# Projecting two blocks of h in each of the first 25 trips of the edge stage, and none in the later ones

## The chip, the cores and the metric

The kernel runs on one core of one Trainium2 chip. The metric is the device time of one execution in microseconds. The cores' engines are TensorE (PE; PEld is its weight load), VectorE (DVE), ScalarE (ACT), GpSimd (POOL) and SyncE (SP), each with its own queue of instructions, which runs in order.

## The reference

One layer of graph attention over N = 6250 nodes of 256 features and E = 200000 edges, sorted by destination, between two layer norms and a feed-forward part. What matters here:

```python
h = jnp.maximum(_layernorm(x, axis=-1), 0.0)
q, k, v = linear(h, wq, bq), linear(h, wk, bk), linear(h, wv, bv)
scores = jnp.sum(q[dst] * k[src], axis=-1) * scale + edge term
attn = softmax of scores over the edges of one dst
out = jax.ops.segment_sum(v[src] * attn[:, None], dst, num_segments=n)
h = layer_norm(h + out + linear(h, ws, bs), g1, b1)      # <- h + linear(h, ws, bs) is the residual
h = layer_norm(h + ffn(h), g2, b2)
return x + h
```

The destinations are `(6250 * uniform ** 2).astype(int)`, sorted. So they are crowded at low numbers: of the 49 blocks of 128 nodes the first holds 56 chunks of 512 edges and the last about 4.

## The kernel before

There are three parts: the first (to about 121 us) normalises x to h, writes h to memory (`h_rows`) and forms q; the edge stage (to about 2078 us) handles all edges; the last part turns the sums into the output.

The edge stage works on chunks of C = 512 edges, 4 tiles of 128. T = 391 chunks hold edges, TP = 392 with the pad. A step is one chunk together with one block of 128 nodes, so a chunk whose edges belong to two blocks takes two steps. A plan made at run time (`steps_tab`) lists the steps, 440 with two empty ones at the end, and the queues run them in 55 trips of U = 8, each trip being one turn of a loop (`eng.Fori(0, n)`) whose body has the eight steps written out. Because the edges are sorted there is one round (`rounds` = 1). Otherwise the same loops would run 49 rounds.

- GpSimd gathers the source rows of a chunk with four indirect DMAs (line 501), each started once a slot of the eight in `rows` is free (`slot_free`). It runs ahead of all others. The first eight chunks are gathered before the stage.
- SyncE waits until the four gathers of a chunk have landed and tells it by `chunk_landed` (L384); it then waits until an older chunk is used up and frees a slot (L388). It also loads the destinations (`dst_of`, L397).
- VectorE multiplies the gathered rows with the q of their destinations (L848, four tiles), takes the running maximum (L902), marks the edges of a block (L715) and adds a step's sums to `acc` (L861).
- ScalarE takes the exponentials (L629, L630), copies their transposes (L633) and prepares the mask of a later step (L596).
- TensorE, in a step: transposes of the exponentials (L1078), the expansion of q to the edges of step s + 2 in two halves (L1025), the spreading of the scores of step s + 1 (L1031), and last the sums of step s (L1091, eight matmuls). The second half of the expansion waits until the products of step s + 1 are done, and those wait for the landing of that step's chunk. So the sums of a step stand behind the landing of the next step's chunk.

Among the steps lies work that has nothing to do with edges: the residual r = h + (h ws + bs) of a block (the identity is added to ws beforehand). A turn of it is

- `turn_h` on TensorE (L1039): two transposes of a block of h, which was loaded before;
- `copy_hTe` on ScalarE: the copy from PSUM (L610) and the load of the next block of h (L611, from `h_rows`);
- `project_h` on TensorE: one bf16 matmul for the bias (L1045) and four for the weights (L1047);
- `copy_r` on ScalarE (L617), and `store_r` (L622): the store to `r_rows`, which the last part reads.

The turns share the upper half of PSUM bank 5, so turn_h waits for the copy_r of the turn before. In every trip of eight steps one turn is done: turn_h behind step 2, copy_hTe behind 3, project_h behind 5, copy_r behind 6, store_r behind 7. The turn's number is r * NW + i with NW = 49, and its block is the number modulo B = 49, so the last six of the 55 turns write blocks 0 to 5 a second time. Where each is issued:

```python
for at, body in ((3, copy_hTe), (6, copy_r), (7, store_r)):   # ScalarE, behind prepare(s + 2, k)
    if steps == U and u == at:
...
if steps == U and u == 2:                                     # TensorE, behind the sums of step u
    turn_h(...)
if steps == U and u == 5:
    project_h(...)
```

At the end SyncE waits until all loads of h and stores of r are done, by a count that the plan writes to `n_trips[3]`.

Of the kernel before, what the change touches and what calls it, by code (L numbers as in the profile page):

```python
# [7 lines left out]
I32 = mybir.dt.int32  # L8
I16 = mybir.dt.int16
ALU = mybir.AluOpType  # L10
# [6 lines left out]
U = 8  # L17
HALF = 4
# [11 lines left out]
def ceil_div(a, b):  # L30
    return -(-a // b)

def gnn_layer(nc, x, src, dst, edge_weight, wq, bq, wk, bk, wv, bv, ws, bs, we, be, g1, b1, g2, b2,
# [9 lines left out]
    B = ceil_div(N, P)  # L44
# [3 lines left out]
    NW = TP // G  # L48
# [12 lines left out]
    MARKED_AT = 40  # L61
    HEAD = ceil_div(T + B, U) * U + 2 * U
# [7 lines left out]
    with ctx:  # L70
        def sb(name, shape, dt=F32):
            return ctx.enter_context(nc.sbuf_tensor(name, shape, dt))
# [33 lines left out]
        n_trips = sb("n_trips", [1, 4], I32)  # L106
# [50 lines left out]
        trips_f, quads_f, last_f, rounds_f = (part(1) for _ in range(4))  # L157
# [154 lines left out]
        def trips(eng, body):  # L312

            n, m, rounds = counts(eng)
            with eng.Fori(0, rounds) as r:
                with eng.Fori(0, n) as i:
                    body(r, i, U)
            with eng.If_lt(eng.to_reg(n), eng.to_reg(n + m)):
                body(0, n, HALF)
# [10 lines left out]
        with nc.Block() as block:  # L330
            @block.sync
            def _(sp):
# [70 lines left out]
                all_turns = sp.alloc_register("all_turns")  # L403
                sp.load(all_turns, n_trips[0:1, 3:4])
                all_back = sp.to_reg(sp.snap(all_turns, min_val=NW, max_val=B * NW) * 16 + 16)
# [113 lines left out]
            def _(act):  # L519
# [104 lines left out]
                def trip(r, i, steps):  # L624
                    first = act.snap(act.to_reg(r * TP + i * U), min_val=0, max_val=B * TP)
                    for u in range(steps):
# [8 lines left out]
                        for at, body in ((3, copy_hTe), (6, copy_r), (7, store_r)):  # L635
                            if steps == U and u == at:
                                body(act.snap(act.to_reg(r * NW + i), min_val=0, max_val=B * NW))
# [5 lines left out]
            def _(dve):  # L643
# [98 lines left out]
                for b in range(B):  # L742
# [49 lines left out]
                    if b == PLAN + 13:  # L792
# [23 lines left out]
                        nc.vector.tensor_scalar(rounds_f[0:1, :], is_sorted[0:1, :], float((1 - B) * NW), float(B * NW), ALU.mult, ALU.add)  # L816
                        nc.vector.tensor_scalar(n_trips[:, 2:3], is_sorted[0:1, :], float(1 - B), float(B), ALU.mult, ALU.add).then_inc(plan, 1)
                        dve.wait_ge(plan, 9)
                        nc.vector.tensor_tensor(n_trips[:, 3:4], trips_f[0:1, :], rounds_f[0:1, :], ALU.add)
# [108 lines left out]
            def _(pe):  # L928
# [139 lines left out]
                def trip(r, i, steps):  # L1068
# [3 lines left out]
                    for u in range(steps):  # L1072
# [20 lines left out]
                        if steps == U and u == 2:  # L1093
                            turn_h(pe.snap(pe.to_reg(r * NW + i), min_val=0, max_val=B * NW))
                        if steps == U and u == 5:
                            project_h(pe.snap(pe.to_reg(r * NW + i), min_val=0, max_val=B * NW))
# [380 lines left out]
```

## Time and profile before

| | |
|---|---|
| median of 3 runs | 2385.33 us (2380.62 to 2385.72) |
| the profiled execution's own time | 2384.42 us |
| its span | 2382.6 us |
| busy over the span: TensorE matmul, weight load | 93%, 78% |
| VectorE, ScalarE, GpSimd | 74%, 49%, 69% |
| edge stage: first sums to last sums start | 121.28 to 2076.09 us |

All times in the rows are counted from the span's start. In a timeline row stand the start, the duration in us, the engine, the line, the operation, output<-input and a count of merged instructions; in brackets the idle time of the engine before it and what released it. "Issue" is time for which the profile shows no wait. Matmuls are pipelined, so starts are compared rather than ends. The clock is the granted share of TensorE's full clock.

### The profile page before, as it was taken

How to read it: one execution, taken by the hardware profiler on the slowest of the kernel's cores; microseconds unless marked ns; L12 is line 12 of the kernel's file. 1: busy time of each engine (PE TensorE's matmuls, PEld its weight loads, DVE VectorE, ACT ScalarE, POOL GpSimd, SP SyncE). 2: the span in 40 equal slices, each digit the busy share in tenths (PEclk: the TensorE clock that was granted, in tenths of full speed). 3: DMA queues.
4: the chain of work that ended last, by engine and by line, in shares of the span. 5: the costliest groups of instructions: out<-in, count | busy, mean ns of one | idle time of the engine just before them, and what ended most of it. 6: DMA issues, size and time to landing. Idle time of an engine off the chain costs nothing. (4 is left out here: it accounts for less than half of the span.)

```text
span 2382.6 us, 69589 instructions
## 1 busy us (share of the span) xinstructions
PE 2210.9 (93%) x14709; PEld 1869.2 (78%) x14710; DVE 1757.8 (74%) x7353; ACT 1164.9 (49%) x2899; POOL 1643.6 (69%) x1828
## 2 busy tenths in 40 slices
PE   6899899899999999999999999999999999999995
PEld 4688777677777777778788888888788888777884
DVE  7777667677667777777777777787787887784378
ACT  5645444444444444444444455555455555463454
POOL 6567777777777777777777777777777777302356
PEclk8999999999999999999999999999999999999997
DMA  8444444444444444444444444444444444340014
GB/s 258 135 135 140 138 137 138 134 135 136 135 138 139 137 138 136 140 137 138 139 136 139 139 139 139 138 139 137 140 136 141 136 140 137 85 147 0 0 55 135
DMA packets 148118, 311.09 MB, mean 131 GB/s; under 512 B 33550, under 2 KB 84609, under 8 KB 148088
## 3 DMA queue, kind: packets, MB, share of 16 engines
q0 software_dynamic: 75264, 205.62, 29.9%
q1 hardware_dynamic: 54702, 90.19, 11.7%
q10 hardware_dynamic: 18122, 14.96, 2.0%
q8 instruction: 9, 0.15, 0.0%
q14 instruction: 21, 0.17, 0.0%
HBM read 290.21 MB, written 20.43 MB: 130 GB/s over the span
## 5 line engine op out<-in xcount | busy, mean ns | idle before, releaser
L501 POOL DMA_INDIRECT work<-h_rows,idx x1536 | 1457.6, 949 | 475.5 <-issue 445.2
L1091 PE MATMUL bank<-work 128*128 x3520 | 837.4, 380 | 0.0
L848 DVE SCALAR_TENSOR_TENSOR work<-bank,work 128x257 bf16<-128x257 f32 x1764 | 647.0, 425 | 223.7 <-SPq L384 191.6
L1025 PE MATMUL bank<-q,onehot 128*128 x5304 | 739.1, 274 | 53.4 <-DVE work L848 50.7
L1091 PEld LDWEIGHTS bank<-work 128*128 128x128 f32 x3520 | 635.3, 190 | 79.2
L1025 PEld LDWEIGHTS bank<-q,onehot 128*128 128x128 bf16 x5304 | 509.9, 98 | 137.5 <-issue 75.9
L633 ACT COPY work<-bank 128x256 f32<-128x256 f32 x880 | 285.5, 377 | 399.3 <-PE bank L1078 397.0
L629 ACT ACTIVATE work<-work 128x1 f32<-128x1 f32 x440 | 129.5, 294 | 619.5 <-DVE work L902 616.6
L902 DVE CUSTOM_DVE_ANT_0 work<-bank,work 128x512 f32<-128x512 f32 x440 | 330.0, 750 | 112.5 <-PE bank L1031 80.6
L630 ACT ACTIVATE work<-work 128x512 f32<-128x512 f32 x440 | 311.5, 708 | 0.0
L1078 PE MATMUL bank<-ident,work 128*128 128x128 f32 x1760 | 267.2, 274 | 30.5 <-ACT work L630 30.5
L1031 PE MATMUL bank<-ident,work 128*128 128x128 f32 x1764 | 272.7, 277 | 15.7 <-DVE work L854 6.9
L596 ACT ACTIVATE work<-onehot 128x512 bf16<-128x512 bf16 x442 | 283.8, 642 | 0.0
L1078 PEld LDWEIGHTS bank<-ident,work 128*128 128x128 f32 x1760 | 213.1, 140 | 87.1 <-ACT work L630 52.8
L1031 PEld LDWEIGHTS bank<-ident,work 128*128 128x128 f32 x1764 | 196.0, 136 | 62.5 <-issue 39.9
L861 DVE SCALAR_TENSOR_TENSOR acc<-acc,work,bank 128x257 f32 x441 | 212.2, 481 | 15.1 <-issue 3.6
L715 DVE TENSOR_SCALAR onehot<-dst_words,node 128x512 bf16 x443 | 166.4, 376 | 68.2 <-issue 36.9
L848 DVE DVE_READ_ACCUMULATOR work<-bank,work 128x1 f32 x1764 | 145.7, 83 | 0.0
L854 DVE TENSOR_TENSOR work<-work,ew_all 128x4 f32<-128x4 f32 x441 | 72.9, 165 | 80.7 <-DVE work L848 39.9
L1273 POOL TENSOR_TENSOR work<-work 128x256 f32<-128x256 f32 x49 | 35.7, 729 | 107.6 <-DVE acc L1349 107.4
L1217 ACT ACTIVATE work<-bank,bff_col 128x128 f32<-128x128 f32 x196 | 55.9, 369 | 104.8 <-PE bank L1428 104.8
L1428 PE MATMUL bank<-work,dst_words 128*128 128x128 f32 x784 | 99.1, 280 | 5.5 <-DVE work L1343 5.5
(192 smaller groups left out, 1594.4 us busy)
## 6 DMA issues: line engine op xcount, KB each, us to landing
dst_words<-dst_short SPq DMA_DIRECT2D x99, 512.0 KB
work<-h_rows,idx POOLq DMA_INDIRECT x1568
bias<-h_rows ACTq DMA_DIRECT2D x56, 128.0 KB
r_rows<-bias ACTq DMA_DIRECT2D x55, 128.0 KB
work<-r_rows SPq DMA_DIRECT2D x49, 128.0 KB, 2.1
acc<-in_x SPq DMA_DIRECT2D x4, 1536.0 KB, 15.6
h_rows<-acc SPq DMA_DIRECT2D x12, 512.0 KB, 6.9
work<-in_x SPq DMA_DIRECT2D x12, 512.0 KB, 3.9
```

The source lines that it names most:

```text
L501: pool.indirect_dma_start(rows[:, u, j, 0:D], None, h_rows, bass.IndirectOffsetOnAxis(idx[:, half, u * J + j:u * J + j + 1], 0)).then_inc( ...
L596: nc.scalar.activation(outside[:, k, :], onehot[:, k].rearrange("p j n -> p (j n)"), ACT.Copy, scale=BIG, bias=-BIG).then_inc(outside_done, 1)
L630: nc.scalar.activation(probsT, masked, ACT.Exp, bias=new_max, scale=-1.0).then_inc(exp_done, 1)
L633: nc.scalar.copy(probs[:, 2 * half:2 * half + 2, :].rearrange("p j n -> p (j n)"), banks[5 - half][:, 0:2 * P]).then_inc(probs_done, 1)
L715: nc.vector.tensor_scalar(onehot[:, k], dst_of[:, bass.ds(at, C)].rearrange("p (j n) -> p j n", j=J), node[:, bass.ds(b, 1)], None, ALU.is ...
L848: last = nc.vector.scalar_tensor_tensor(out=product[:, j, 0:D1], in0=banks[j][:, 0:D1], scalar=SCALE, in1=rows[:, bass.ds(slot, 1), j, :], ...
L861: nc.vector.scalar_tensor_tensor(out=a, in0=a, scalar=decay[:, k:k + 1], in1=banks[6 + k][:, 0:D1], op0=ALU.mult, op1=ALU.add).then_inc(ad ...
L902: nc.vector.tensor_tensor_reduce(out=masked, in0=banks[4][:], in1=outside[:, k, :], scale=-1.0, scalar=old_max[:, k:k + 1], op0=ALU.add, o ...
L1025: last = nc.tensor.matmul(banks[j][:, 0:D1], onehot[:, k, j, :], q3[:, bass.ds(b, 1), c, 0:D1], start=(c == 0), stop=(c == 2))
L1031: last = nc.tensor.transpose(banks[4][:, j * P:(j + 1) * P], score[:, k, j:j + 1].broadcast_to([P, P]), ident[:])
L1078: last = nc.tensor.transpose(banks[5 - half][:, j * P:(j + 1) * P], probsT[:, (2 * half + j) * P:(2 * half + j + 1) * P], ident[:])
L1091: last = nc.tensor.matmul(banks[6 + k][:, 0:D1], probs[:, j, :], rows[:, bass.ds(slot, 1), j, :], start=(j == 2), stop=(j == 1))
```

## The change

`trips` gets two loops in place of one, for TensorE and ScalarE: the first runs trips 0 to PROJECTED - 1 (PROJECTED = ceil(49 / 2) = 25) with the body that projects, the second runs trips 25 to 54 with a body that does not. The projecting body has two turns, numbered (r * 25 + i) * 2 and one more: turn_h behind steps 0 and 4, copy_hTe behind 1 and 5, project_h behind 2 and 6, copy_r and store_r both behind 3 and 7. There are 50 turns instead of 55 (the last writes block 0 a second time). VectorE's loop, GpSimd's and SyncE's are not touched; the plan on VectorE drops two operations on one element, and SyncE's last count is worked out from a constant.

```diff
--- before.py
+++ after.py
@@ -59,6 +59,7 @@
     BY_ACT = 14
     PLAN = 16
     MARKED_AT = 40
+    PROJECTED = ceil_div(B, 2)
     HEAD = ceil_div(T + B, U) * U + 2 * U
     TRIPS = ceil_div(T + B, U)
     TG = ceil_div(T, P)
@@ -103,7 +104,7 @@
         eps = sb("eps", [P, 1])
         node = sb("node", [P, NB])
         neg_max = sb("neg_max", [P, NB])
-        n_trips = sb("n_trips", [1, 4], I32)
+        n_trips = sb("n_trips", [1, 3], I32)
         steps_tab = sb("steps_tab", [1, HEAD], I32)
         free_tab = sb("free_tab", [1, TP + LEAD], I32)
         idx_all = sb("idx_all", [P, R], I32)
@@ -154,7 +155,7 @@
         ends, firsts = part(TG), part(TG)
         falls = part(1)
         is_sorted = part(1)
-        trips_f, quads_f, last_f, rounds_f = (part(1) for _ in range(4))
+        trips_f, quads_f, last_f = (part(1) for _ in range(3))
         trips_i, quads_i = (part(1, I32) for _ in range(2))
         node_i = part(NB, I32)
 
@@ -313,10 +314,15 @@
 
             n, m, rounds = counts(eng)
             with eng.Fori(0, rounds) as r:
-                with eng.Fori(0, n) as i:
-                    body(r, i, U)
+                with eng.Fori(0, PROJECTED) as i:
+                    body(r, i, U, True)
+                with eng.Fori(PROJECTED, n) as i:
+                    body(r, i, U, False)
             with eng.If_lt(eng.to_reg(n), eng.to_reg(n + m)):
-                body(0, n, HALF)
+                body(0, n, HALF, False)
+
+        def turn_of(eng, r, i, k):
+            return eng.snap(eng.to_reg((r * PROJECTED + i) * 2 + k), min_val=0, max_val=B * 2 * PROJECTED)
 
         def block_of(eng, step):
             return eng.snap(eng.to_reg(step & (BLOCKS - 1)), min_val=0, max_val=B)
@@ -400,9 +406,7 @@
                 last = sp.to_reg(rounds * (2 * 16 * NW) + 16)
                 sp.wait_ge(late_in, 7 * 16)
                 sp.wait_ge(dst_in, last)
-                all_turns = sp.alloc_register("all_turns")
-                sp.load(all_turns, n_trips[0:1, 3:4])
-                all_back = sp.to_reg(sp.snap(all_turns, min_val=NW, max_val=B * NW) * 16 + 16)
+                all_back = sp.to_reg(rounds * (2 * PROJECTED * 16) + 16)
                 sp.wait_ge(late_in, 7 * 16)
                 sp.wait_ge(h_back, all_back)
                 sp.wait_ge(late_in, 7 * 16)
@@ -621,7 +625,7 @@
                     act.wait_ge(r_copied, turn + 2)
                     act.dma_start(r_rows[bass.ds(turn % B * P, P), :], r_out).then_inc(r_stored, 16)
 
-                def trip(r, i, steps):
+                def trip(r, i, steps, projecting):
                     first = act.snap(act.to_reg(r * TP + i * U), min_val=0, max_val=B * TP)
                     for u in range(steps):
                         s, k = first + u, u % 2
@@ -632,9 +636,9 @@
                             act.wait_ge(turned, s * 2 + (2 - half))
                             nc.scalar.copy(probs[:, 2 * half:2 * half + 2, :].rearrange("p j n -> p (j n)"), banks[5 - half][:, 0:2 * P]).then_inc(probs_done, 1)
                         prepare(s + 2, k)
-                        for at, body in ((3, copy_hTe), (6, copy_r), (7, store_r)):
-                            if steps == U and u == at:
-                                body(act.snap(act.to_reg(r * NW + i), min_val=0, max_val=B * NW))
+                        for at, body in ((1, copy_hTe), (3, copy_r), (3, store_r), (5, copy_hTe), (7, copy_r), (7, store_r)):
+                            if projecting and u == at:
+                                body(turn_of(act, r, i, u // 4))
 
                 act.wait_ge(plan_done, 1)
                 trips(act, trip)
@@ -813,10 +817,8 @@
                         dve.wait_ge(plan, 8)
                         nc.vector.tensor_scalar(trips_f[0:1, :], trips_f[0:1, :], -float(NW), is_sorted[0:1, 0:1], ALU.add, ALU.mult)
                         nc.vector.tensor_scalar(n_trips[:, 1:2], last_f[0:1, :], is_sorted[0:1, 0:1], None, ALU.mult)
-                        nc.vector.tensor_scalar(rounds_f[0:1, :], is_sorted[0:1, :], float((1 - B) * NW), float(B * NW), ALU.mult, ALU.add)
                         nc.vector.tensor_scalar(n_trips[:, 2:3], is_sorted[0:1, :], float(1 - B), float(B), ALU.mult, ALU.add).then_inc(plan, 1)
                         dve.wait_ge(plan, 9)
-                        nc.vector.tensor_tensor(n_trips[:, 3:4], trips_f[0:1, :], rounds_f[0:1, :], ALU.add)
                         nc.vector.tensor_scalar(n_trips[:, 0:1], trips_f[0:1, :], float(NW), None, ALU.add).then_inc(plan, 1)
                     if b == PLAN + 17:
                         most = TP + LEAD
@@ -1065,7 +1067,7 @@
                 pe.wait_ge(dotted, 2)
                 expand_q(1, 1, ahead[1])
 
-                def trip(r, i, steps):
+                def trip(r, i, steps, projecting):
                     pe.load(regs[0:steps + 2], steps_tab[0:1, bass.ds(i * U, steps + 2)])
                     first = pe.snap(pe.to_reg(r * TP + i * U), min_val=0, max_val=B * TP)
                     step_of = [pe.snap(v, min_val=0, max_val=(TP + U + HALF) * BLOCKS) + r * ROUND for v in regs[0:steps + 2]]
@@ -1090,10 +1092,10 @@
                                 pe.wait_ge(probs_done, s * 2 + 2)
                             last = nc.tensor.matmul(banks[6 + k][:, 0:D1], probs[:, j, :], rows[:, bass.ds(slot, 1), j, :], start=(j == 2), stop=(j == 1))
                         last.then_inc(summed, 1)
-                        if steps == U and u == 2:
-                            turn_h(pe.snap(pe.to_reg(r * NW + i), min_val=0, max_val=B * NW))
-                        if steps == U and u == 5:
-                            project_h(pe.snap(pe.to_reg(r * NW + i), min_val=0, max_val=B * NW))
+                        if projecting and u in (0, 4):
+                            turn_h(turn_of(pe, r, i, u // 4))
+                        if projecting and u in (2, 6):
+                            project_h(turn_of(pe, r, i, u // 4))
 
                 trips(pe, trip)
```

## Rows read from the trace of the kernel before

**Rows 1.** The page, first part: busy time of each engine.

```profile
PE 2210.9 (93%) x14709; PEld 1869.2 (78%) x14710; DVE 1757.8 (74%) x7353; ACT 1164.9 (49%) x2899; POOL 1643.6 (69%) x1828
```

**Rows 2.** Windows of 100 us, L501 alone: us, busy (count), clock, DMA.

```profile
400.00:500.00 100.00, 75.68 (x80) 1.00 0.46 137
...
1900.00:2000.00 100.00, 75.53 (x80) 1.00 0.47 139
```

**Rows 3.** A window, all engines: PE, PEld, DVE, ACT, POOL busy, clock, DMA.

```profile
1900.00:2000.00 100.00, 98.82 (x691) 86.56 (x691) 80.18 (x361) 51.56 (x126) 75.97 (x82) 1.00 0.47 139
```

**Rows 4.** Timeline, GpSimd: first and last gather of the edge stage.

```profile
124.60 0.94 POOL L501 DMA_INDIRECT work<-h_rows,idx  x1 [14.74 <-SPq L388]
...
2052.82 0.95 POOL L501 DMA_INDIRECT work<-h_rows,idx  x1 [0.30 <-issue]
```

**Rows 5.** Waits, 500 to 900, then 1700 to 2080: total us, times, longest.

```profile
DVE work L848 <- SPq L384: 65.6, 54, 2.5
...
DVE work L848 <- SPq L384: 5.9, 4, 2.5
```

**Rows 6.** Timeline, TensorE: sums of successive steps in a late trip.

```profile
1887.78 1.90 PE L1091 MATMUL bank<-work 128*128 x8
...
1891.94 1.90 PE L1091 MATMUL bank<-work 128*128 x8
...
1899.82 1.90 PE L1091 MATMUL bank<-work 128*128 x8
...
1904.74 1.90 PE L1091 MATMUL bank<-work 128*128 x8
...
1908.68 1.90 PE L1091 MATMUL bank<-work 128*128 x8
...
1913.36 1.90 PE L1091 MATMUL bank<-work 128*128 x8
```

**Rows 7.** Timeline: last sums on TensorE, and VectorE behind its loop.

```profile
2076.09 1.90 PE L1091 MATMUL bank<-work 128*128 x8
2079.57 0.48 DVE L861 SCALAR_TENSOR_TENSOR acc<-acc,work,bank 128x257 f32 x1 [3.36 <-issue]
```

**Rows 8.** Timeline, TensorE: first sums of trip 0 and of trip 25.

```profile
121.28 2.51 PE L1091 MATMUL bank<-work 128*128 x8
...
1050.38 1.90 PE L1091 MATMUL bank<-work 128*128 x8
```

**Rows 9.** Timeline: a chunk's fourth gather and the sums behind it, twice.

```profile
1203.88 0.94 POOL L501 DMA_INDIRECT work<-h_rows,idx  x1 [0.30 <-issue]
...
1208.99 0.95 POOL L501 DMA_INDIRECT work<-h_rows,idx  x1 [0.30 <-issue]
...
1210.31 1.90 PE L1091 MATMUL bank<-work 128*128 x8
...
1215.01 1.90 PE L1091 MATMUL bank<-work 128*128 x8
```

**Rows 10.** Line L622, the store of r: duration ns min/median/max, first, last.

```profile
L622 ACTq FUSED_REGOPS  x55: 91/91/97, 149.4 to 2074.7; - x55
...
L622 ACTq DMA_DIRECT2D r_rows<-bias x55: 362/362/398, 149.5 to 2074.9; - x55
```

**Rows 11.** Timeline, ScalarE: the exponential behind the copy of r.

```profile
1220.36 0.29 ACT L629 ACTIVATE work<-work 128x1 f32<-128x1 f32 x1 [0.78 <-DVE work L902]
```

**Rows 12.** Tile bias (it holds h_in, hT_e and r_out): landings of its loads.

```profile
DMA to landing us min/median/max: 6.5/6.9/8.3
```

**Rows 13.** DMA queues from 200 to 2070 us: packets, MB, share.

```profile
q0 software_dynamic: 70896, 193.69, 35.9%
q1 hardware_dynamic: 13248, 48.24, 7.8%
q10 hardware_dynamic: 15120, 13.77, 2.3%
```

**Rows 14.** A short window: PE, PEld, DVE, ACT, POOL busy, clock, DMA.

```profile
320.50:323.90 3.40, 3.40 (x14) 2.67 (x13) 2.98 (x15) 0.91 (x2) 2.74 (x3) 0.50 0.38 105
```

## The prediction

> **What bounds the kernel now.** I read the page first. TensorE is busy 93% of the span and GpSimd 69% [rows 1], and that would name TensorE. Shares of a whole span hide stages, so the edge stage (about 121 to 2078 us of the 2382.6) was read next, in windows of 100 us. GpSimd's gathers stand at 80 in 100 us both early and late, 75.7 and 75.5 us busy [rows 2], while TensorE, 93% over the span, is at 98.8 us of 100 in the late window, at the full clock [rows 3]. So the engine that is only three quarters busy keeps one constant pace all along, and the other fills up late. The rest of GpSimd's time is the 0.30 us ahead of every gather, put down to issue, so it has no room: from the first gather of the stage at 124.60 to the last at 2052.82 [rows 4] there are 1536, 1.256 us each, and four of them fetch a chunk: **5.02 us per chunk**. The view of waits says who feels it: VectorE's product (L848) waited for SyncE's word that a chunk had landed (L384) 54 times, 65.6 us, between 500 and 900, but 4 times, 5.9 us, after 1700 [rows 5].
>
> The reason lies in the data. A step is one chunk with one block of nodes. There are 440 steps in 55 trips of 8 (with two empty ones at the end) but 392 chunks (391 of edges), and a chunk at the border of two blocks takes two steps. The destinations of the reference fall as the square of a uniform number, so early blocks hold some 56 chunks and late ones 4. Counting the reference's destinations, trips 0 to 24 (200 steps) use 189 chunks and trips 46 to 53 (64 steps) use 52. For GpSimd these last 64 steps are 52 x 5.02 = 261 us.
>
> What TensorE needs without waits is read from the late trip whose last-of-step matmuls (L1091) start at the times in [rows 6]. A plain step takes 1908.68 - 1904.74 = 3.94, **3.945 us** in the mean. The step behind the two transposes of turn_h takes 1891.94 - 1887.78 = 4.16, so turn_h costs **0.21 to 0.22**. The step behind project_h takes 1904.74 - 1899.82 = 4.92, so project_h costs **0.97**. The first step of a trip takes 1913.36 - 1908.68 = 4.68, so a loop's turn costs **0.73**. A trip with one projection is 8 x 3.945 + 0.73 + 0.22 + 0.97 = **33.5 us**. The last 64 steps before trip 54 then take TensorE 268 us, where the gathers take 261. TensorE is the bound there and falls behind. The last gather is over at 2052.82 + 0.95 = 2053.77, but the last step's matmuls begin only at 2076.09 [rows 4, 7]. Up to about trip 44 the gathers are the bound, from there TensorE.
>
> **The change, part by part.** (1) Two projections in each of trips 0 to 24. TensorE needs 31.56 + 0.73 + 2 x 1.19 = 34.7 us a trip, 867 us for 25. These trips took 1050.38 - 121.28 = 929 us from first sums to first sums [rows 8], so 62 us, 2.5 per trip, lie idle and cover it: cost nothing. If that cover were gone it would cost 25 x 1.19 = 30 us. The first four trips have no such room, since eight chunks stand ready at the start and TensorE works them off at its own pace. It comes 4 x 1.19 = 5 us later there and then meets the gathers' pace anyway. GpSimd is not held meanwhile: the gather of chunk 32 at about 245 us needs step 24 summed, whose sums are due at 121.3 + 3 x 34.7 = 225.4 and over 1.9 later, so some 17 us are to spare.
>
> (2) No projections in trips 25 to 54. A trip is 31.56 + 0.73 = **32.3 us**. The 64 steps are now 258 us against the gathers' 261, so the lag no longer builds up and **the last landing sets the end**. The fourth gather of a chunk that starts at 1208.99 ends at 1209.94, and the sums of the step ahead of that chunk's start at 1215.01, 5.07 us later, for they wait behind its product. A slower case is 1204.82 to 1210.31, 5.49 [rows 9]. Chunk 391 is first used by step 438, so the sums of step 437 start at 2053.77 + 5.07 = 2058.8, and those of step 439 two plain steps later, at 2066.7. Earlier chunks give nearly the same bound. Chunk 383 is over eight chunks earlier, at 2013.6; step 427's sums at 2018.7; twelve steps and one loop turn later, 2066.8. A recurrence over all 440 steps (the later of the step before plus its price and of its chunk's landing plus 3.2) gives 2067.1. The same recurrence for the kernel before gives 2075.1, where the trace has 2076.09 [rows 7]. Part of that 1 us is landings in the TensorE-bound trips that now count less, so I take 2067.5. **The stage ends 8.6 us earlier.** Bounds: 2066.7 at the best (9.4 us). At the worst the slow landing (+0.4), the whole error of the recurrence (+1.0) and one stretch of half clock in the last steps (+1.7, below) make 2070.2 (5.9 us).
>
> (3) Five projections fewer (50 for 55), with their 5 loads of h and 5 stores of r [rows 10]. Their TensorE time is among what (2) takes out. The traffic falls by 1.3 MB of 311 and no step waits for it. Nothing more is counted.
>
> (4) ScalarE does the same two copies of 0.37 us, twice per trip now. Behind the copy at 1219.20 it waits 0.78 us for VectorE, until 1220.36 [rows 11]. store_r moves from the trip's last step to right behind copy_r, so ScalarE's queue waits for its own copy and then issues the store. The issue takes 0.36 and the register work ahead of it 0.09 [rows 10], 0.45 in all, and 0.78 covers it. If it did not, the next exponentials would start late by the rest, in the first 25 trips alone, where (1) has 2.5 us a trip. What is queued behind on ScalarE is that step's L629 and L630, and TensorE's transposes wait for those. The load of the next h is issued one step behind turn_h and needed three steps later. That is at least 11.8 us, where loads of that tile landed in 6.5 to 8.3 us [rows 12]. The store has four steps to land. Both bounds: nothing, and 25 x 2 x 0.1 = 5 us, all of it inside the 62.
>
> (5) A second body on the queues of TensorE and ScalarE. No instruction fetch is in the trace between 200 and 2070 us (its queues are absent from the list of those 1870 us [rows 13]), so the repeated bodies stay at hand. Entering the new one at trip 25 costs between nothing and the 3.36 us that VectorE stood in issue when it left its loop at the stage's end [rows 7]. I take 3. GpSimd does not wait for it, and a 7-chunk trip gives back 35.1 - 32.3 = 2.8 us, so it is gone after two trips: nothing at the end. VectorE, GpSimd and SyncE keep their loops. Two one-element operations of the plan go, under 0.3 us beside TensorE's work: nothing.
>
> The Trainium skill, Perfetto Trace Analysis, section Identifying the Most-Contended Engine, says to take the engine with the highest occupancy as the bound, with TensorE judged by its weight loads. Here that is TensorE at 93% and 78%. By that page only the five dropped projections count, and rival A says what they are worth; the constant 80 gathers per 100 us speak against it.
>
> **The sum.** The profiled execution took 2384.42 us, 1.8 around the span of 2382.6, and lies 0.9 under the median 2385.33. What follows the stage (304 us) is unchanged and starts when the last sum is done. 2384.4 - 8.6 = 2375.8. I say **2376.0**, 0.39% faster than the median.
>
> **Rivals.**
> A: TensorE sets the pace of the whole stage, so that moved projections are worth nothing and dropped ones 5 x 1.19 = 6.0 us: 2378.4. For it: 93% busy. Against it: [rows 2, 5]. Chance 0.03.
> B: the tail gives part back, within 0.2%. After the change TensorE has short idle stretches late too. In trips 4 to 24 the clock fell once with such stretches, at 320.5, to 0.50 (1.2 GHz) for 3.4 us [rows 14], which costs 1.7 us of its work. In the last 16 steps nothing covers that. Three of them, or one and a stretch of half clock longer than before in the part behind (there were three of about 6.8 us, worth 3.4 each), leave under 4.8 us of the gain: about 2381. Against it: one in 21 trips. Chance 0.11.
> C: slower. The second body of TensorE is not kept and is fetched anew each trip. Price: up to 3.4 us for each of 30 trips (the exit at the stage's end). In the recurrence 0.95 us per trip cancels most of the gain (2072.5), 1.5 makes it zero (2077.1), and 3.4 ends the stage at 2117, at **2425 us** overall. Against it: the body of before is longer by the projection and was not fetched [rows 13]. Chance 0.04. The Trainium skill, Runtime: NRT & Kernel Launch, section Instruction fetch mechanics, says that a taken branch to a target outside the window of pages held forces a fetch before the engine goes on. [...] The trace agrees only in that nothing is fetched while the loops of before turn.
> D: slower. Two projections stall the first trips beyond their room, a load of h landing late above all. In the recurrence 4 us more per trip still costs nothing at the end and 8 us costs 69: 2453. Against it: 8.3 us where 11.8 are there. Chance 0.02.
> E: the new split is not run. The plan's other path (49 rounds, unsorted) projects by other counts; but 55 projections are in the trace [rows 10], so the sorted path is. Within 0.2%, chance 0.02.
> My forecast has 0.78.
>
> **Range.** A measurement of this kernel can tell about 0.2% (4.8 us) from no change; three runs spread over 5.1. Low: 2384.4 - 9.4 - 3.4 (one stretch of half clock less behind the stage) = 2371.6. High: 2384.4 - 5.9 + 3.4 = 2381.9. It takes in A and most of B and leaves out C and D. Of the forecast's 0.78 some 0.73 lies beyond 0.2%, with A's 0.02: faster 0.75. Within: 0.05 + 0.01 + 0.11 + 0.02 = 0.19. Slower: 0.06.
>
> **What the profile after would show.** GpSimd's 1536 gathers start and end as before (2052.8). TensorE's transposes of turn_h are 100, the last by 1055 us. VectorE waits for landings (L384) late in the stage too, tens of times after 1700. Steps in the last trips are 3.95 us or held by a landing, and the last L1091 starts at 2067 to 2068. L1091's first step costs 4.7 at a loop's turn, not more. I am wrong if the gathers come later than before, if TensorE's late trips stay at 33.5, or if its gaps at the loop's turn grow.

## The result, and the profile after

| | before | after |
|---|---|---|
| median (7 runs each, same chip) | 2385.15 us (2380.62 to 2387.18) | 2378.11 us (2375.56 to 2380.54) |
| ratio, 95% interval | | 0.9969 [0.9958, 0.9981] |
| profiled execution, its span | 2384.42, 2382.6 us | 2378.11, 2376.3 us |
| end of the last gather | 2053.77 us | 2055.02 us |
| start of the last sums | 2076.09 us | 2070.69 us |
| from there to the end of the span | 306.5 us | 305.6 us |

Faster by 0.3%, 7.0 us by the medians and 6.3 between the two profiled executions. Of the 6.3, the stage gives 2076.09 - 2070.69 = 5.4 and the part behind it 0.9. In kernel.py of after the gather is L505, SyncE's word of a landing L390, the product L850, the sums L1093, the expansion of q L1027 and turn_h L1041.

The page, first part, answers to [rows 1]; it moves hardly at all, because five projections are 6 us of 2200.

```profile
PE 2203.8 (93%) x14674; PEld 1861.0 (78%) x14675; DVE 1756.2 (74%) x7351; ACT 1162.2 (49%) x2889; POOL 1644.9 (69%) x1828
```

What moved is in the waits from 1700 to 2080 us, which answer to the second line of [rows 5]: VectorE now stands 21 times for a landing late in the stage, 20.3 us, where it stood 4 times for 5.9.

```profile
DVE work L850 <- SPq L390: 20.3, 21, 2.9
```

The projections all lie in the first 25 trips. The lines view of turn_h's line (duration in ns min/median/max, first and last start) counts 100 transposes, the last at 1035.1 us:

```profile
L1041 PE MATMUL bank<-ident,bias x100: 271/272/273, 123.3 to 1035.1; 128*128 128x128 f32 x100
```

The end of the stage is where the forecast's size is decided. Timeline of after, the last gather, the last sums on TensorE, and the product that TensorE waited for:

```profile
2054.07 0.95 POOL L505 DMA_INDIRECT work<-h_rows,idx  x1 [0.30 <-issue]
...
2056.45 1.90 PE L1093 MATMUL bank<-work 128*128 x8
...
2059.74 0.43 DVE L850 SCALAR_TENSOR_TENSOR work<-bank,work 128x257 bf16<-128x257 f32 x1 [2.90 <-SPq L390]
...
2062.81 1.90 PE L1093 MATMUL bank<-work 128*128 x8
...
2066.75 1.90 PE L1093 MATMUL bank<-work 128*128 x8
...
2070.69 1.90 PE L1093 MATMUL bank<-work 128*128 x8
```

The last sums stand 2070.69 - 2055.02 = 15.7 us behind the last gather, where they stood 2076.09 - 2053.77 = 22.3 behind it [rows 4, 7]. Step 437 took 2062.81 - 2056.45 = 6.36 us in place of 3.94: VectorE's product waited 2.90 us for the landing of the last chunk, and TensorE stood behind it. That chunk's word came at 2059.6, 4.57 us behind its fourth gather, where I had read 1.9 from ordinary chunks (the 5.07 of the prediction less the 3.2 from a landing to the sums). How far the last sums stand behind the last gather is the measure for all the runs below, because the gathers' own end moved between 2053.4 and 2059.4 us from profile to profile, with the same 1536 gathers.

The early trips have not become longer for their second projection. The sums of step 200, the first of trip 25, start where they did in [rows 8], 1050.56 for 1050.38:

```profile
1050.56 1.90 PE L1093 MATMUL bank<-work 128*128 x8
```

The instruction queue shows two packets between 200 and 2070 us, where [rows 13] has none, both in the first trip of the second body:

```profile
q8 instruction: 2, 0.03, 0.0%
```

### The profile page after: what moved, and what is told of

It is laid out like the page before. It is cut to its first block and busy times, and to the rows that moved or that the text cites. A ratio compares the mean times of both kernels' runs of the same rounds, so it can differ in the third digit from the quotient of the medians.

```text
span 2376.3 us, 69443 instructions
## 1 busy us (share of the span) xinstructions
PE 2203.8 (93%) x14674; PEld 1861.0 (78%) x14675; DVE 1756.2 (74%) x7351; ACT 1162.2 (49%) x2889; POOL 1644.9 (69%) x1828
## 5 line engine op out<-in xcount | busy, mean ns | idle before, releaser
L505 POOL DMA_INDIRECT work<-h_rows,idx x1536 | 1459.0, 950 | 478.6 <-issue 443.1
L1093 PE MATMUL bank<-work 128*128 x3520 | 836.7, 380 | 0.0
L850 DVE SCALAR_TENSOR_TENSOR work<-bank,work 128x257 bf16<-128x257 f32 x1764 | 646.8, 425 | 246.2 <-SPq L390 216.1
L1027 PE MATMUL bank<-q,onehot 128*128 x5304 | 738.9, 274 | 54.9 <-DVE work L850 52.4
L1093 PEld LDWEIGHTS bank<-work 128*128 128x128 f32 x3520 | 634.8, 190 | 79.0
L1027 PEld LDWEIGHTS bank<-q,onehot 128*128 128x128 bf16 x5304 | 508.7, 98 | 139.8 <-issue 77.1
L1033 PEld LDWEIGHTS bank<-ident,work 128*128 128x128 f32 x1764 | 195.3, 136 | 66.3 <-issue 38.8
L850 DVE DVE_READ_ACCUMULATOR work<-bank,work 128x1 f32 x1764 | 145.5, 82 | 0.0
## 6 DMA issues: line engine op xcount, KB each, us to landing
acc<-in_x SPq DMA_DIRECT2D x4, 1536.0 KB, 15.7
```

The lines of the kernel that those rows point to most:

```text
L505: pool.indirect_dma_start(rows[:, u, j, 0:D], None, h_rows, bass.IndirectOffsetOnAxis(idx[:, half, u * J + j:u * J + j + 1], 0)).then_inc( ...
L850: last = nc.vector.scalar_tensor_tensor(out=product[:, j, 0:D1], in0=banks[j][:, 0:D1], scalar=SCALE, in1=rows[:, bass.ds(slot, 1), j, :], ...
L1027: last = nc.tensor.matmul(banks[j][:, 0:D1], onehot[:, k, j, :], q3[:, bass.ds(b, 1), c, 0:D1], start=(c == 0), stop=(c == 2))
L1033: last = nc.tensor.transpose(banks[4][:, j * P:(j + 1) * P], score[:, k, j:j + 1].broadcast_to([P, P]), ident[:])
L1093: last = nc.tensor.matmul(banks[6 + k][:, 0:D1], probs[:, j, :], rows[:, bass.ds(slot, 1), j, :], start=(j == 2), stop=(j == 1))
```

## The experiments

The theory, called G in the expectations: the gathers set the pace to about trip 44, TensorE the rest, so only projections in the late trips cost time. The rival T: TensorE sets the pace of the whole stage, so every projection costs the same wherever it stands. A third, M: the moving and doubling itself matters, not only the dropping.

**A first set that drowned.** In these kernels the values from the plan that waits and addresses use are bounded first: a mask on each, and a maximum on some.

```diff
-            return eng.snap(eng.to_reg(step >> (BLOCKS.bit_length() - 1)), ...)
+            return eng.snap(eng.to_reg((step >> (BLOCKS.bit_length() - 1)) & 0xFFFFF), ...)
```

The kernel before, so bounded, was to be the zero:

> The kernel before, with the values that are loaded from memory held non-negative ahead of every wait (three register maxima at the head of each queue's loop, one AND more in the register work of VectorE's chunk number and of SyncE's counts). Every kernel of these experiments carries it, so this one is their zero. Expected by both theories: no change, 2385 us (within 2), last sums (L1091 of before) starting near 2076, gathers unchanged at 5.02 us per chunk.

Measured: 2550.29 us against 2385.06, ratio 1.0691 [1.0676, 1.0705]. That is not a zero. The three comparisons that were built on it, whose edits are shown with the second set, came out with it:

> The change turned round: trips 0 to 29 project nothing, trips 30 to 54 project two blocks each, 50 projections as in the changed kernel. Theory G (gathers set the pace but for the last ten trips, where TensorE does): the recurrence puts the last sums at 2091.9 where before has 2076.1, so about 16 us slower than before, 2401 us. Theory T (TensorE sets the pace of the whole stage, a projection costs 1.19 us wherever it stands): 5 fewer than before, 6 us faster, 2379.

> One projection per trip as before, but none in trips 0 to 4: 50 in trips 5 to 54, the same number as in the changed kernel, the five dropped at the early end. Theory G: no gain, the early trips wait for gathers anyway: 2385 us, last sums at 2075 to 2076. Theory T: 5 x 1.19 = 6 us faster, 2379.

> One projection per trip in trips 0 to 48 at the places of before (behind steps 2 and 5), none in trips 49 to 54: only the six that are not needed are dropped, nothing is moved or doubled. Theory G: the lag that TensorE still builds up in trips 45 to 48 is worked off in the last six, and the last landing sets the end as in the changed kernel: last sums at 2069.4 to 2070.7, 2378 us, equal to the changed kernel. A theory that the moving does it (late trips must all be free, as in the diff) has it gain at most part: 2381 to 2384.

Measured, in the same order: late 2503.7 (1.0486 [1.0462, 1.051]), skip_first 2548.67 (1.0682 [1.0667, 1.0697]) and once_49 2544.08 (1.0669 [1.0654, 1.0683]). The cause is on the page of b_held, the third part, where the queue that fetches VectorE's instructions has 291 packets for 21 in before. Between 200 and 2070 us the same view has 241 for none:

```profile
q14 instruction: 291, 2.38, 0.3%
...
q14 instruction: 241, 1.97, 0.3%
```

The trace, which also holds the register instructions, counts 353 instructions of VectorE per trip in place of 321. Once per trip VectorE stands in issue ahead of its running maximum, 3.3 us in the mean and 4.4 at the most over the 18 trips from 1200 to 1900 us. The first line is from the waits of b_held, the others from its timeline, where ScalarE stands behind VectorE:

```profile
DVE work L907 <- issue: 59.6, 18, 4.4
...
1205.16 0.75 DVE L907 CUSTOM_DVE_ANT_0 work<-bank,work 128x512 f32<-128x512 f32 x1 [4.38 <-issue]
...
1205.95 0.29 ACT L634 ACTIVATE work<-work 128x1 f32<-128x1 f32 x1 [6.32 <-DVE work L907]
```

This set says nothing on G or T for the kernel before, because the stall makes another kernel of it. b_held needs 38.8 us for each of trips 0 to 29 (first sums to first sums), where before needs 36.9 at the gathers' pace. GpSimd itself waits for free slots there (85.4 us from 1200 to 1900, where before has 2.1). So the gathers are no longer what holds the early trips, and a projection costs there too: late, which has none in these trips, takes 37.4 and comes out 47 us under b_held. It does show what rival C of the prediction would have looked like, had the change caused it: hundreds of packets, not two.

**The same bound without an instruction.** Here the plan's three tables are 16-bit without sign, so that the values cannot be negative, in the changed kernel.

```diff
-        n_trips = sb("n_trips", [1, 3], I32)
-        steps_tab = sb("steps_tab", [1, HEAD], I32)
-        free_tab = sb("free_tab", [1, TP + LEAD], I32)
+        n_trips = sb("n_trips", [1, 3], U16)
+        steps_tab = sb("steps_tab", [1, HEAD], U16)
+        free_tab = sb("free_tab", [1, TP + LEAD], U16)
```

> The changed kernel with its three small tables (n_trips, steps_tab, free_tab) kept as unsigned 16-bit numbers in place of 32-bit ones, so that what the queues load from them can't be negative and no instruction is added. The four runs before grew VectorE's loop body by register work (321 instructions a trip became 353) and instruction fetches turned up in every trip (241 packets between 200 and 2070 us where before has none), which swamped what they were to measure. Expected if the body's size was their cause: no fetches in the stage, ratio 0.997 as the changed kernel, 2378 us. If it was the held registers or the waits themselves: slower than before by per cents again.

Measured: 2408.42 against 2387.2, ratio 1.0089 [1.0072, 1.0106]. No fetch but the two packets that after has as well, and yet slower, by a wait of VectorE that before does not have. Waits of after_u16, 1200 to 1900 us, 2.1 us once per trip:

```profile
DVE work L857 <- issue: 41.3, 20, 2.1
```

The tables' type is all that was changed, and the load of a trip's values from `steps_tab` into VectorE's registers shows it. The view of its line, in after_u16 and then in after, has 2.71 us for a load in place of 0.86 (duration in ns min/median/max):

```profile
L873 DVEq TENSOR_LOAD <-steps_tab x55: 2704/2710/2960, 149.5 to 2095.0; - x55
...
L872 DVEq TENSOR_LOAD <-steps_tab x55: 848/855/873, 147.8 to 2067.9; - x55
```

**The second set.** The bounds are now maxima, written so that they add no instruction to VectorE's loop: the trace of before_m has 440 more fused register operations on VectorE, eight per trip, and 440 fewer waits as instructions of their own. So VectorE has its 321 instructions per trip again.

```diff
-                    dve.wait_ge(chunk_landed, there)
+                    dve.reg_alu(landed_held, there, 0, ALU.max)
+                    dve.wait_ge(chunk_landed, landed_held)
```

> The kernel before, with the loaded values held non-negative by maxima that are packed into register instructions that are there already: VectorE's loop body keeps its count of instructions (289 as written, 321 in a trip of the trace). If the growth of the body caused the slow runs of the first set: no instruction fetches between 200 and 2070 us, 321 instructions per trip on VectorE, 2385 us (within 3). If the maxima themselves cost: VectorE's steps longer, slower by over 0.5%.

> The changed kernel with the same maxima. Against before_m the difference should be that of the changed kernel against the kernel before: 7 us, last sums at 2070 to 2071 against 2076 to 2077. The landing of the last chunk (391, which is all padding and fetches one and the same row 512 times) should again come some 4.5 us behind its fourth gather, where others take 1.9, and hold the last three steps: the sums of step 437 start 3.2 us behind that landing.

Measured: before_m 2384.03 against 2384.92, ratio 0.9999 [0.999, 1.0008]; after_m 2377.45, ratio 0.9971 [0.9961, 0.9981]. No instruction packet is in the trace of before_m between 200 and 2070 us. This form is a zero, and the change keeps its gain in it. The last sums stand 22.0 us behind the last gather in before_m and 15.1 in after_m.

**The two projections late.** The same 50 projections in pairs, in trips 30 to 54 in place of 0 to 24:

```diff
-                with eng.Fori(0, PROJECTED) as i:
-                    body(r, i, U, True)
-                with eng.Fori(PROJECTED, n) as i:
-                    body(r, i, U, False)
+                with eng.Fori(0, LATE) as i:          # LATE = 30
+                    body(r, i, U, False)
+                with eng.Fori(LATE, n) as i:
+                    body(r, i, U, True)
```

> With the maxima of before_m: trips 0 to 29 project nothing, trips 30 to 54 two blocks each, 50 projections as in the changed kernel. Theory G (the gathers set the pace up to about trip 44 and TensorE only behind it): the recurrence puts the last sums at 2091.9 against 2075.1 for before, 16 to 17 us slower than before_m, 2401 us; last sums 37 to 39 us behind the end of the last gather. Theory T (TensorE sets the pace of the whole stage, a projection costs 1.19 us wherever it stands): five fewer, 6 us faster, 2378.

Measured: 2395.75 against 2388.2, ratio 1.003 [1.0019, 1.0042]: slower, though five projections fewer are made. T has it faster and falls. The last sums start 31.3 us behind the last gather, 9.3 more than in before_m. G has the sign and not the size (37 to 39). Sums of late_m, the last step of a trip and around it:

```profile
1906.07 1.90 PE L1103 MATMUL bank<-work 128*128 x8
1910.01 1.90 PE L1103 MATMUL bank<-work 128*128 x8
1914.93 1.90 PE L1103 MATMUL bank<-work 128*128 x8
1919.27 1.90 PE L1103 MATMUL bank<-work 128*128 x8
```

project_h costs 1914.93 - 1910.01 = 4.92, as in [rows 6]. But the step at the loop's turn behind it takes 4.34 here, not 4.68 (4.1 to 4.6 over trips 38 to 54). Twice two transposes and projections with it make 8 x 3.945 + 2 x 1.19 + 0.40 = 34.3 us per trip, not 34.7; its trips show 34.1 to 34.6. Trips 37 to 53, seventeen of them, together take 5.8 us less than 17 times 34.7. That is most of the 6 to 8 us by which G was too high. A reason can be read from VectorE's rows. First before, then late_m, at the same place of a trip:

```profile
1907.88 0.35 DVE L715 TENSOR_SCALAR onehot<-dst_words,node 128x512 bf16 x1 [0.73 <-issue]
1910.98 0.65 PE L1078 MATMUL bank<-ident,work 128*128 128x128 f32 x4 [0.41 <-ACT work L630]
```

```profile
1913.18 0.39 DVE L728 TENSOR_SCALAR onehot<-dst_words,node 128x512 bf16 x1 [0.75 <-issue]
1917.02 0.65 PE L1090 MATMUL bank<-ident,work 128*128 128x128 f32 x4 [0.19 <-issue]
```

The 0.73 us of the loop's turn are in the main VectorE's, which stands 0.7 us in issue at its own turn, and TensorE feels them through the exponentials (0.41 on L630). Where project_h lies behind the seventh step (u = 6), TensorE comes to that point 0.97 later and waits 0.19, which is most of the 0.34 between 4.68 and 4.34. So the two costs overlap, as far as these two places show it, and the sum of step prices that I made for a pair was 0.35 us too high per trip.

**The first five left out.** Placement of before, one projection per trip, in trips 5 to 54:

```diff
+                with eng.Fori(0, FREE) as i:          # FREE = 5
+                    body(r, i, U, False)
+                with eng.Fori(FREE, n) as i:
+                    body(r, i, U, True)
```

> With the maxima: one projection per trip as before, none in trips 0 to 4, 50 in trips 5 to 54. Theory G: nothing gained, 2384 us, last sums 22 us behind the end of the last gather as in before_m. Theory T: 5 x 1.19 = 6 us faster, 2378, like the changed kernel, which has the same number.

Measured: 2388.91 against 2388.2, ratio 1.000 [0.9991, 1.0009]; 22.5 us behind the last gather. The same number of projections as in the change brings nothing when the five are dropped early. The trace shows where their time goes: from the sums of step 0 to those of step 24 it is 98.8 us in place of the 101.3 of before_m, but to those of step 200 it is 929.1 in place of 928.8. This is rival A refuted by a run.

**One per trip to the 49th, none behind.** Placement of before, trips 0 to 48, none in 49 to 54; nothing is moved or doubled:

```diff
-    PROJECTED = ceil_div(B, 2)
+    PROJECTED = NW                                   # 49
```

> With the maxima: one projection per trip in trips 0 to 48 at the places of before, none in trips 49 to 54; nothing is moved or doubled. Theory G: TensorE's lag of trips 45 to 48 is worked off in the last six, and the landing of chunk 391 sets the end: last sums 15 to 16 us behind the end of the last gather, 2377 us, equal to after_m. Theory M (the doubling in the early trips and 30 free ones are what gains): at most part of it, 2380 to 2383.

Measured: 2381.4 against 2388.2, ratio 0.997 [0.9958, 0.9983], as the change has; 15.3 us behind the last gather. Theory M falls as the account of the gain: leaving out the six late turns, which computed blocks 0 to 5 a second time, gives all of what the change gives. That is not all that late projections cost: the last two kernels below show what the four in trips 45 to 48 cost besides, behind the slow landing.

**Other rows for the pads.** The chunk that lands late is chunk 391, all of it padding: its 512 entries name the same row 0 of h. In pads_m, built on the changed kernel, they name rows 0 to 127 in each tile:

```diff
-                nc.vector.memset(src_i[:, FULL_G, :], 0)
+                pool.iota(src_i[:, FULL_G, :], [[1, P]], base=0, channel_multiplier=0).then_inc(pads_set, 1)
```

> after_m with the padding's source indices 0, 1, 2, ... 127 in each gather in place of 0 throughout, so that the last chunk and the padded part of the one before fetch 128 rows instead of one and the same. If the one row is why chunk 391 lands 4.5 us behind its gather, it lands 1.9 behind it, the sums of step 437 start 5.1 behind the gather's end, the last sums 13.0 to 13.6 us behind it (15.1 in after_m), 2 us faster than after_m, 2375.5. If the late landing has another cause (the end of GpSimd's queue, SyncE's order): no change, 2377.5.

Measured: the chunk lands 1.84 us behind its fourth gather (4.57 in after), the product that waits for it waits 0.44, and no step is held; steps are 3.94 apart to the end and the last sums start 13.0 us behind the last gather (2059.41). Timeline of pads_m:

```profile
2058.46 0.95 POOL L512 DMA_INDIRECT work<-h_rows,idx  x1 [0.30 <-issue]
...
2060.59 1.90 PE L1102 MATMUL bank<-work 128*128 x8
2061.42 0.43 DVE L859 SCALAR_TENSOR_TENSOR work<-bank,work 128x257 bf16<-128x257 f32 x1 [0.44 <-SPq L394]
...
2064.53 1.90 PE L1102 MATMUL bank<-work 128*128 x8
...
2068.47 1.90 PE L1102 MATMUL bank<-work 128*128 x8
...
2072.41 1.90 PE L1102 MATMUL bank<-work 128*128 x8
```

So the slow landing comes of naming one row over and over: neither the end of GpSimd's queue nor SyncE's order was changed. In the time (2380.38 against 2388.2, ratio 0.9962 [0.9948, 0.9975]) it lies 0.0008 below once_49_m, less than the intervals tell apart: the 2 us are shown in the trace and not in the medians.

**No step on the padding chunk.** A last kernel, on once_49_m: the plan lets the two empty steps use the last chunk with edges.

```diff
-                        nc.vector.tensor_scalar(row(sorted_k), row(sorted_k), float(TP - 1), None, ALU.min)
+                        nc.vector.tensor_scalar(row(sorted_k), row(sorted_k), float(T - 1), None, ALU.min)
```

> The kernel of once_49_m (the placement of before, 49 projections in the first 49 trips, none after), and besides the plan gives the two empty steps behind the last edges the last chunk that holds edges (390) in place of the all-padding chunk 391. Chunk 391 is still gathered, but no step waits for it. Theory G (the end of the stage hangs on a chunk's landing, and in the runs so far on the slow landing of chunk 391): the last sums start at TensorE's own pace, 13.0 to 14 us behind the end of the last gather, as in pads_m (13.0), in place of 15.1 to 15.7; chunk 391 itself still lands 4.0 to 4.6 us behind its gather; TensorE's steps 437 to 439 are 3.95 apart; the time is 1.5 to 2.5 us under that of once_49_m against the same kernel before: a ratio of 0.996, about 2376 to 2379. If the last steps are slow for another cause (the empty steps themselves, or the stage's exit), the last sums stay 15 to 16 behind and the ratio at 0.997.

Measured: 2379.22 against 2384.99, ratio 0.9975 [0.9966, 0.9984]. Chunk 391 lands 4.06 us behind its gather and no one waits: the last steps are 3.94 apart, as G says. But the last sums start 15.1 us behind the last gather, not 13 to 14, and the time is not better. Timeline of once_49_last_m, then of once_49_m:

```profile
2052.45 0.95 POOL L511 DMA_INDIRECT work<-h_rows,idx  x1 [0.30 <-issue]
...
2056.68 1.90 PE L1102 MATMUL bank<-work 128*128 x8
...
2060.61 1.90 PE L1102 MATMUL bank<-work 128*128 x8
...
2064.55 1.90 PE L1102 MATMUL bank<-work 128*128 x8
...
2068.49 1.90 PE L1102 MATMUL bank<-work 128*128 x8
```

```profile
2060.44 1.90 PE L1102 MATMUL bank<-work 128*128 x8
2065.02 1.90 PE L1102 MATMUL bank<-work 128*128 x8
```

My expectation had taken the base wrongly. In once_49_m the landing holds step 437 by only 4.58 - 3.94 = 0.64 us, for TensorE itself is late there: from step 357 on each of its steps runs at the plain price, or at 4.7 at the loop's turn, 4.17 behind turn_h and 4.92 behind project_h (the last at step 390), so four projections in trips 45 to 48 still count. In the changed kernel, which has none there, the same landing holds it by 2.42. The two kernels reach the same 15 us by different roads, and each edit that removes one road's last wait leaves the other. With the slow landing out of the way on both, the last sums stand 13.0 us behind the last gather where the late projections are moved (pads_m) and 15.1 where four of them stay (this kernel). So moving is worth about 2 us over dropping, by two single profiles, and the slow landing of the padding chunk hides it in the changed kernel. The changed kernel with no step on the padding chunk was not run; pads_m is the nearest to it. No kernel here beats the changed one by more than the intervals.

## Why the prediction was right, and where its size was off

**The bound, and (1).** Right. Pairs in the first 25 trips cost nothing that reaches the end: trip 25 starts within 0.2 us of where it did. On the other side, pairs late (late_m) cost 9.3 us at the stage's end against one per trip, and five early ones dropped (skip_first_m) bring nothing.

**(2) The end of the stage.** The mechanism is right: late trips take 32.3 us where no landing holds them, TensorE is no longer behind, and a landing sets the end. The size was 8.6 us and the trace has 5.4. The step that failed is the term "+5.07", the distance from the last gather to the sums ahead of its chunk, which I took from chunks in mid-stage. Measured, it is 2062.81 - 2055.02 = 7.79. Chunk 391 names one row 512 times and lands 4.57 us behind its gather, not 1.9, and the +0.4 that the worst case had for a slow landing was too small as well. Step 437 took 6.36 us for it, 2.42 over a plain step; pads_m shows the 2.42 gone. The other part is the gathers' end, 2055.02 for 2053.77, 1.25 later. The forecast of "as before (2052.8)" for the last gather's start missed by that. Together: 2070.69 - 2.42 - 1.25 = 2067.0, where the prediction had 2067.1 to 2067.5. The slow landing was in the rows of before: there the chunk landed 4.37 us behind its gather, hidden by TensorE's own lag of 22.3 us. The view of SyncE's word in before, from 2055 to 2062 us, has it (rounded; 4.37 us behind 2053.77 is 2058.14):

```profile
L384 SPq EVENT_SEMAPHORE  x1: 28/28/28, 2058.1 to 2058.1; - x1
```

I had looked at landings only where they were waited for, and those are other chunks than the one that would become the last wait.

**The 1.25 us.** The prediction says that it is wrong if the gathers come later than before, and by these two profiles they do. But that sign asked more of a single profile than it can tell, and the 1.25 us is not the change's doing so far as the runs show. Over before, after and the seven kernels of the second set and behind it, the first gather starts at 122.8 to 125.6 us and the last ends at 2053.4 to 2059.4, and kernels with the old placement lie among the others (2055.4 in before_m, 2053.7 in skip_first_m, 2053.9 in after_m). A difference of two single profiles carries this noise. The distance behind the last gather moves by much less (22.0 to 22.5 us with the old placement, 15.1 to 15.7 with the new).

**(3), (4).** Nothing of them shows. The counts are as said (100 transposes, none behind 1035.1 us).

**(5) The second body.** Two packets were fetched at 1054 and 1070 us, in the first trip of the second body, and none after. I took 3 us for the entry and the trace shows no price at all: of the steps there, the one from 1054.51 to 1059.78 is long, but VectorE's product in it waited 1.81 us for a landing, as in any trip of that part.

```profile
1056.71 0.43 DVE L850 SCALAR_TENSOR_TENSOR work<-bank,work 128x257 bf16<-128x257 f32 x1 [1.81 <-SPq L390]
```

The price didn't enter the sum, so nothing hung on it. Rival C is refuted by the two packets. The Trainium skill, Runtime: NRT & Kernel Launch, section Instruction fetch mechanics, has a taken branch outside the held pages pay a fetch; the trace of after has the fetches in the new body's first trip but no wait for them, and b_held has the stall at every turn of a loop that has grown, with 241 packets and 165 us.

**Behind the stage.** I had it unchanged; it was 0.9 us shorter, in a part that took 303.8 to 306.9 us over the runs with nothing changed in it. Rival B, that the tail gives back to within 0.2%, didn't come about (ratio 0.9969). Of the 8.6 us expected at the stage's end 3.2 were lost, but to a landing and to the gathers' end, not to the clock. The windows of after from 121 to 2065 us, and of before from 121 to 2070, in order of the columns of [rows 3], have the clock at 1.00 both times, and those behind it (from 2065, and from 2070) at 0.93 both times. After:

```profile
121.00:2065.00 1944.00, 1849.96 (x12599) 1567.88 (x12599) 1460.74 (x6564) 937.08 (x2287) 1469.78 (x1584) 1.00 0.46 137
2065.00:2376.30 311.30, 264.62 (x1622) 224.02 (x1619) 201.22 (x502) 152.85 (x409) 107.83 (x148) 0.93 0.22 67
```

**The late pair's price.** The 34.7 us per trip of (1) was 0.35 too high, as late_m shows, on the safe side; trips 1 and 2 of after, where TensorE works at its own pace, take 34.2 and 34.3. It comes of adding step prices that were each read alone, though one of them is a wait on VectorE that the other covers.

**The time.** 2376.0 was forecast, 2378.11 measured: the 8.6 less its two misses, 2.42 and 1.25, with 0.5 and 0.9 on the other side, are the 6.3 between the profiles.

## What to carry to other kernels

Shares of busy time said TensorE, and it was the bound in only the first three and the last ten or so of 55 trips; ask of each stretch which wait ends last, and put the optional work where the other engine is the bound. Dropping the surplus late work was worth as much here as moving all of it, so ask first what is computed twice. When a bound falls away, read the next one at the very instruction that will carry it (the last chunk's own landing, not a typical one), because a lag can hide an oddity of just that one. And in a kernel whose loop bodies are long, count the instructions of an edit before trusting it as an experiment.

## What the runs showed of the hardware that was not expected

- Four gathers of 128 entries that all name one row landed 3.9 to 4.6 us behind the last of them in before, after and the kernels of the second set but late_m, where it was 6.4. With 128 different rows each (pads_m) it was 1.84 us. Ordinary chunks took 1.9. In late_m a load of destinations and a store of r were issued at 2051.16 and 2052.20 us, among these four gathers, where in the others the last such issue lies over six us ahead of them. That this makes the 6.4 was not tested.
- Thirty-two more instructions in VectorE's loop body (321 to 353 by the trace) brought 241 instruction packets between 200 and 2070 us and a stall of 3.3 us in the mean each turn, and 165 us in all over the kernel before. Replacing instructions one for one cost nothing (ratio 0.9999).
- The load of a trip's values into registers of VectorE took 2.71 us from a table of 16-bit values and 0.86 us from one of 32-bit values (medians of 55).
- A second loop body on TensorE and ScalarE cost two packets in its first trip and no time that can be read.
